# One counting round fewer before a top-k threshold, and half of the masking products on another engine

## What is computed

```python
scores = jnp.einsum('bqd,bkd->bqk', q, k) / math.sqrt(c)
k_keep = max(1, int(KEEP * n))                       # int(0.1 * 1024) = 102
topk_vals, topk_idx = jax.lax.top_k(scores, k_keep)
mask = jnp.full_like(scores, neg_inf)
mask = mask.at[bi, qi, topk_idx].set(topk_vals)
attn = jax.nn.softmax(mask, axis=-1)
out = jnp.einsum('bqk,bkd->bqd', attn, v)
```

## Time and profile before

| | us |
|---|---|
| median of three runs | 1622.19 (1621.81 to 1622.51) |
| the profiled execution | 1619.43 |
| its span on the core | 1617.7 |
| DVE busy | 1310.6 (81%) |
| PE busy | 1255.3 (78%) |
| POOL busy | 924.1 (57%) |
| ACT busy | 916.9 (57%) |

### The profile page before, as it was taken

One profiled execution on the slowest core, in us unless ns is written; L12 is line 12 of the kernel. 1 busy time (PEld: TensorE's weight loads), 2 busy tenths in 40 slices (PEclk: granted clock), 3 DMA queues, 4 the chain that ended last, 5 costly groups with the idle time before them and its releaser, 6 DMA issues. The chain is left out here.

```text
span 1617.7 us, 17563 instructions
## 1 busy us (share of the span) xinstructions
PE 1255.3 (78%) x4450; PEld 644.4 (40%) x4450; DVE 1310.6 (81%) x1519; ACT 916.9 (57%) x1270; POOL 924.1 (57%) x487
## 2 busy tenths in 40 slices
PE   3308788898865778889973879888986668888868
PEld 1106253343525344334441625343452624434343
DVE  2785899998697699999678589999869678999930
ACT  1705767575644566666481575757564565656712
POOL 2122568787181547868345257878618164887834
PEclk8658789999987879999996878999998786999989
DMA  2000012221020012222021011222102001222203
GB/s 71 13 1 1 30 52 101 81 91 65 32 87 14 2 41 91 91 85 92 20 92 40 1 30 52 104 78 91 65 26 80 14 2 47 88 101 78 91 14 118
DMA packets 30498, 91.92 MB, mean 57 GB/s; under 512 B 4790, under 2 KB 8764, under 8 KB 30428
## 3 DMA queue, kind: packets, MB, share of 16 engines
q1 hardware_dynamic: 30428, 91.10, 16.2%
HBM read 88.34 MB, written 2.75 MB: 56 GB/s over the span
## 5 line engine op out<-in xcount | busy, mean ns | idle before, releaser
L637 POOL TENSOR_TENSOR work<-expo,ring 128x1024 f32<-128x1024 f32 x128 | 299.9, 2363 | 126.6 <-DVE expo L1295 124.6
L637 POOL TENSOR_TENSOR ring<-ring 128x1024 f32<-128x1024 f32 x128 | 299.8, 2365 | 9.8 <-DVE ring L1295 9.8
L1295 DVE TENSOR_TENSOR_SCAN expo<-ring,ps 128x1024 f32<-128x1024 f32 x128 | 286.0, 2270 | 0.0
L1745 PE MATMUL ps<-ring,ident 128*128 128x512 f32 x512 | 262.5, 617 | 28.0 <-POOL ring L637 21.5
L1295 DVE TENSOR_TENSOR_SCAN ring<-ring,ps 128x1024 f32<-128x1024 f32 x128 | 284.1, 2261 | 0.0
L1745 PE MATMUL ps<-work,ident 128*128 128x512 f32 x512 | 241.1, 593 | 0.0
L887 ACT ACTIVATE ring<-dt_f,decay 128x1024 f32<-128x1024 f32 x128 | 146.6, 1148 | 105.4 <-DVE expo L1295 61.5
L681 ACT ACTIVATE b_dtx_tok<-dtx_tok,b_tok 128x256 f32<-128x256 f32 x448 | 189.2, 493 | 0.0
L1708 PE MATMUL ps<-ident,b_dtx_tok 128*128 128x128 f32 x896 | 122.2, 279 | 46.4 <-DVE expo L1295 42.3
L1708 PEld LDWEIGHTS ps<-ident,b_dtx_tok 128*128 128x128 f32 x896 | 95.9, 140 | 138.8 <-issue 69.6
L1745 PEld LDWEIGHTS ps<-ring,ident 128*128 128x128 f32 x512 | 82.8, 189 | 166.2 <-POOL ring L637 128.1
(11 more groups left out here) (271 smaller groups left out, 2243.2 us busy)
## 6 DMA issues: line engine op xcount, KB each, us to landing
ring<-c_rows SPq DMA_DIRECT2D x128, 512.0 KB, 3.5
b_dtx_tok<-comb_rows SPq DMA_DIRECT2D x32, 512.0 KB, 3.6
x_c<-in_x SPq DMA_DIRECT2D x4, 512.0 KB, 3.3
out<-xs_f SPq DMA_DIRECT2D x4, 512.0 KB, 2.6
w<-in_L_ffn_w SPq DMA_DIRECT2D x2, 512.0 KB
ring<-in_L_attn_f_in_proj_w SPq DMA_DIRECT2D x1, 256.0 KB
ring<-in_L_attn_b_in_proj_w SPq DMA_DIRECT2D x1, 256.0 KB
c_rows<-dbc_f SPq DMA_DIRECT2D x4, 64.0 KB, 1.9
```

The source lines that it names most:

```text
L637: pool.tensor_tensor(hc[odd][:, k, :], hs[odd][:, k, :], c_all[:, odd, :], ALU.mult).then_inc(hc_ready, 1)
L1295: v.tensor_tensor_scan(hs[odd][:, k, order], dA[:, k, order], dbu[:, order], 0.0, ALU.mult, ALU.add).then_inc(scan_ready, 1)
L1745: last = mm(halves(ps[2 * k])[h], ident[:, :], hc[odd][:, k, h * BANK:(h + 1) * BANK], start=False, stop=stop)
```

## The change

Three rounds of counting become two, with another rule for the second correction. It weights the second step by the sizes of both steps (`SECANT` is 0.8) instead of by a fixed factor. The last count, with the mask, is done by ACT for all eight tiles. Of the masking products, those of tiles 4 to 7 are made by DVE, straight from score and threshold (`lower`), and those of tiles 0 to 3 stay on POOL. The ladder takes tiles 4 to 7 first and then 0 to 3. ACT copies the threshold to the ladder's head. `ranks` comes behind the ladder. The first two exponentials need only six tiles of the ladder to be done, and stand ahead of `result` in ACT's list.

```diff
-    DAMPING = (1.0, 0.6, 0.5)
-    COUNTS = len(DAMPING) + 1
+    SECANT = 0.8
+    COUNTS = 3
...
-        low_scores = [work[:, 0, :], work[:, 1, :], expo[:, 0, :], expo[:, 1, :]]
+        ladder_order = list(range(ACT_TILES, TILES)) + list(range(ACT_TILES))
+        low_scores = [(expo[:, 0, :], expo[:, 1, :], work[:, 0, :], work[:, 1, :])[j % 4] for j in range(TILES)]
...
-                pool.wait_ge(laddered, b * TILES + max(j - 3, 0))
-                pool.tensor_tensor(low_scores[j % 4], score[:, j, :], below[j], ALU.mult).then_inc(masked, 1)
+                pool.wait_ge(counted, b * COUNTED + 2 * ACT_TILES + j + 1)
+
+                pool.wait_ge(laddered, b * TILES + j + 1)
+                pool.tensor_tensor(low_scores[j], score[:, j, :], below[j], ALU.mult).then_inc(masked, 1)
...
+            def count_last(b, tiles):
+
+                act.wait_ge(thresh_ready, (b + 1) * COUNTS)
+                for i in tiles:
+                    nc.scalar.activation(below[i], score[:, i, :], ACT.Sign, bias=thresh[:, i:i + 1], scale=-1.0,
+                                         accum_out=count[:, i:i + 1]).then_inc(counted, 1)
+
+            def copy_base(b):
+
+                act.wait_ge(thresh_ready, (b + 1) * COUNTS)
+                copy(ladder[:, :, 0], thresh[:, :]).then_inc(base_copied, 1)
...
-                act.wait_ge(laddered, (b + 1) * TILES)
+                act.wait_ge(laddered, b * TILES + TILES - 2)
...
-                count_signs(b, 2)
                 if m is not None:
                     gelu(m, 3)
+                count_last(b, range(ACT_TILES))
+                if m is not None:
                     gelu(m, 4)
-                count_signs(b, 3)
-                if m is not None:
-                    for x in range(5, EXPERTS):
-                        gelu(m, x)
-                    result(m)
+                copy_base(b)
+                if m is not None:
+                    gelu(m, 5)
+                count_last(b, range(ACT_TILES, TILES - 2))
+                if m is not None:
+                    gelu(m, 6)
+                count_last(b, range(TILES - 2, TILES))
+                if m is not None:
+                    gelu(m, 7)
                 exponent(b, 0)
                 exponent(b, 1)
+                if m is not None:
+                    result(m)
...
+            def first_correction(b):
+
+                correct(b, 0)
+                v.scalar_tensor_tensor(neg_thresh[:, :], delta[:, :], -1.0, neg_thresh[:, :],
                                        ALU.mult, ALU.add).then_inc(thresh_ready, 1)
-                link(v.scalar_tensor_tensor(thresh[:, :], delta[:, :], DAMPING[c], thresh[:, :],
-                                              ALU.mult, ALU.add))
-                if c == COUNTS - 2:
-                    dve.sem_inc(thresh_ready, 1)
+                v.scalar_tensor_tensor(first_move[:, :], delta[:, :], -1.0, delta[:, :], ALU.mult, ALU.max)
+                link(v.tensor_tensor(thresh[:, :], delta[:, :], thresh[:, :], ALU.add))
+
+            def second_correction(b):
+
+                correct(b, 1)
+                v.tensor_tensor(moves[:, :], delta[:, :], first_move[:, :], ALU.mult)
+                link(v.scalar_tensor_tensor(weight[:, :], delta[:, :], -1.0, delta[:, :], ALU.mult, ALU.max))
+                link(v.scalar_tensor_tensor(weight[:, :], first_move[:, :], 1 / SECANT, weight[:, :], ALU.mult,
+                                            ALU.add))
+                link(v.reciprocal(weight[:, :], weight[:, :]))
+                link(v.tensor_tensor(moves[:, :], moves[:, :], weight[:, :], ALU.mult))
+                link(v.tensor_tensor(thresh[:, :], moves[:, :], thresh[:, :], ALU.add))
+                dve.sem_inc(thresh_ready, 1)
+
+            def lower(b):
+
+                for n, j in enumerate(range(ACT_TILES, TILES)):
+                    v.scalar_tensor_tensor(low_scores[j], score[:, j, :], thresh[:, j:j + 1], score[:, j, :],
+                                           ALU.is_lt, ALU.mult).then_inc(lowered, 1)
```

More of the change, by code:

```diff
@@ L117, in hybrid_block @@
         correction = sb("correction", [P, TILES])
+        first_move = sb("first_move", [P, TILES])
+        moves = sb("moves", [P, TILES])
+        weight = sb("weight", [P, TILES])
         thresh = sb("thresh", [P, TILES])
@@ L651, in pool_image @@
                     expert_residual(m)
-                    for x in range(4):
+                    for x in range(5):
                         select(m, x)
[L654 to L657, removed]
+                mask_score(b, 0)
+                mask_score(b, 1)
+                if m is not None:
+                    select(m, 5)
+                    select(m, 6)
+                mask_score(b, 2)
+                mask_score(b, 3)
+                if m is not None:
+                    select(m, 7)
                 layer_norm(b)
@@ L994, in _ @@
             v.tensor_scalar(flat_w, flat_w, 0.5, None, ALU.mult).then_inc(setup_scaled, 1)
[L996 removed]
+            begin, end, step, after, link, steps_now = step_counter(dve, vstep, 4 + 4 + 2 * COUNTS + 2 * (TILES - ACT_TILES) + 6 * TILES + 1)
             begin_tail, end_tail, step_tail, after_tail, link_tail, _ = step_counter(dve, tstep, 9 + 2 * TILES)
@@ L1060, in count_above @@
                                          ALU.is_ge, ALU.add, accum_out=count[:, i:i + 1]))
[L1062 to L1066, removed]
             def correct(b, c):
                 after(0)
-                dve.wait_ge(counted, (b * COUNTS + c + 1) * ACT_TILES)
+                dve.wait_ge(counted, b * COUNTED + (c + 1) * ACT_TILES)
                 v.scalar_tensor_tensor(delta[:, by_sign], count[:, by_sign], N - 2 * TARGET,
@@ L1095, in first_below @@
+            def first_below(b, pair):
+                for n in pair:
+                    j = ladder_order[n]
+                    if n < 4:
+                        dve.wait_ge(lowered, b * 4 + n + 1)
+                    else:
+                        dve.wait_ge(masked, b * ACT_TILES + j + 1)
                     passed(dve)
-                    step(v.max(ladder[:, j, 1:9], low_scores[j % 4]))
+                    step(v.max(ladder[:, j, 1:9], low_scores[j]))
             def next_below(b, pair):
-                for j in pair:
+                for n in pair:
+                    j = ladder_order[n]
@@ L1101, in next_below @@
                     after()
-                    step(v.match_replace(low_scores[j % 4], ladder[:, j, 1:9], low_scores[j % 4], REPLACED))
-                for j in pair:
-                    after(pair[1] - j)
-                    v.max(ladder[:, j, 9:17], low_scores[j % 4]).then_inc(laddered, 1)
+                    step(v.match_replace(low_scores[j], ladder[:, j, 1:9], low_scores[j], REPLACED))
+                for n in pair:
+                    j = ladder_order[n]
+                    after(pair[1] - n)
+                    v.max(ladder[:, j, 9:17], low_scores[j]).then_inc(laddered, 1)
@@ L1497, in dve_image @@
                     next_below(b, (j, j + 1))
+                ranks(b)
                 resolve(b)
```

44 lines of the change are left out of this document (15 added, 29 removed).

## The result

Four runs of the changed kernel have a median of 1601.37 us (1599.59 to 1602.81), four of the kernel before 1622.35 us (1621.81 to 1623.28). The ratio is 0.9872, with a 95% interval of 0.9859 to 0.9884. The forecast of 1603.5 us is 2.1 us too high, and the time lies in its range. The profiled execution took 1599.59 us, with a span of 1597.8 us, which is 19.9 less than before.

A forecast was written before the change was run, and what follows sets the result against it. The prediction took DVE to bound the threshold search. Gains of 7.4 us in image 0 and 11.3 us in images 1 to 3, 18.7 us off 1622.19, gave 1603.5 us, range 1593 to 1611.

The forecast's parts named there:

- the holds: Images 1 to 3: POOL's selects hold second-correction instructions and `lower`, 2.35 us each; none to two in `lower`, chance 0.81.
- The rule in the prediction: Threshold search: a DVE instruction with two SBUF tensors, or such a copy, waits until POOL's two-tensor instruction ends; 2.02 to 2.32 us.

The follow-up runs named there:

- e_hold1: The changed kernel with POOL starting select 1 only once DVE's four products are done, and selects 4 to 7 moved behind masks: 1580.29 us, ratio 0.9744.
- e_changed_again: The same file as the changed kernel, timed again in the second group of runs: 1602.13 us, ratio 0.9883 to the kernel before.
- e_missed: The changed kernel with SECANT 1e-6 in place of 0.8, so that rows are missed and `exact` runs: 2552.64 us in its one execution.

## What to carry to other kernels

Before a large two-input instruction is moved to the vector engine, look which GpSimd products can start in its time, and order them by a semaphore: one wait in GpSimd's list, with slack behind it, was worth 11 to 21 us here, as much as the change itself. (`e_hold1`, the best of the three, also moves three selects further behind the masks.) A shortened stage moves what follows under other work, so a cut must be priced at its new place: the same round was worth 4.6 us in one image and nothing in another. Ties within 0.3 us can go either way: even in the same file, run twice, the holds fell on other instructions (`moves` in image 1 of the changed kernel, `thresh` in `e_changed_again`). So put both outcomes into the range, and don't credit or blame an edit for them.

## What the runs showed of the chip that I hadn't expected

- **The size doesn't matter for a hold.** A 128x1 instruction of 0.15 us took 2.33 us, a 128x8 one 2.17: the length is what is left of POOL's product. The counts, which read one tensor and write their sum, kept their 1.20 us through every select.
- **Nor does it take two tensors.** Forms that read one tensor and write no sum are held too: the copy at L1089 (2.10 us), and the `TENSOR_SCALAR` of `ranks`, 0.92 us in image 3 of the kernel before, where the like one behind it takes 0.16, and 0.69 in image 1 of `e_hold1` instead of 0.15. Each ends with a POOL product. The rule in the prediction names the copy, but not this form.
- **The branch is dear where it jumps.** The kernel holds the attention stage behind the search twice, once with tests and `exact` for each tile and once without. With no row missed, the branch passes over the first. That leaves DVE 3.41 us of "issue" ahead of the first masked exponential in image 0 of the changed kernel (2.93 in the earlier trace rows):

```profile
112.31 1.28 DVE L1206 SCALAR_TENSOR_TENSOR expo<-ring,kept_from,expo 128x1024 f32<-128x1024 f32 x1 [3.41 <-issue]
```

In `e_missed`, where the same branch falls through into `exact`, the copy shown above starts after 0.66 us. In image 3 there it falls through too, and then skips one `exact`, since tile 0 has no missed row:

```profile
1971.18 1.29 DVE L1206 SCALAR_TENSOR_TENSOR expo<-ring,kept_from,expo 128x1024 f32<-128x1024 f32 x1 [1.34 <-issue]
```

So the jump over the whole stage costs 2.70 to 3.45 us in the changed kernel's four images, and that over one `exact` less. No run changes the branch alone, so what in the jump takes the time stays open.

- **The start has two lengths.** In the changed kernel the first count starts at 56.69 us, in `e_hold1` at 58.66, with the same work ahead. From 35 to 41.5 us the granted clock of PE is 0.88 in the one and 0.50 (its lower level, 1.2 GHz) in the other, and PE gets through 11 and 7 matmuls. The changed kernel (columns as in the first fence):

```profile
35.00:41.50 6.50, 5.39 (x11) 1.81 (x10) 1.42 (x3) 1.66 (x2) 0.00 (x0) 0.88 0.00 0
```

And `e_hold1`:

```profile
35.00:41.50 6.50, 5.39 (x7) 1.75 (x7) 0.00 (x0) 1.02 (x1) 0.00 (x0) 0.50 0.00 0
```

What decides this isn't shown. It is 2 us, enough to mislead whoever compares spans only: the 22.6 us that `e_hold1` gains in the stretches over the changed kernel are 17.1 in the spans. Of the difference 2.0 are this start, 0.9 the held `ranks` of images 1 and 2, and 3.0 lie behind the last image's first masked exponential, where the two kernels do the same work. The last of these isn't explained. Some 0.4 go the other way.
